# Value-row expansion on GpSimd's queue, a later residual fold, one joined block and edge lists in parts in a fused convolution, attention and graph kernel

## The chip, the cores and the metric

The kernel runs on one core of one Trainium2 chip. The core has five engines with a queue of instructions each: TensorE (PE, matmuls and transposes), VectorE (DVE), ScalarE (ACT), GpSimd (POOL) and SyncE (SP). DMAs are issued from the queues of SP, ACT and POOL. The metric is the device time of one execution in microseconds (us); lower is better.

## The reference, cut to what matters

The input is x, 8 images of 56 x 56 pixels with 64 channels, in float32. Three layers follow one another.

```python
# layer 0: 32 paths, each 1x1 to 4 channels, 3x3, 1x1 back to 64 (batch norm and relu after each)
x = relu(sum_over_paths(path(x)) + x)
t = x.reshape(8, 3136, 64)
# layer 1: attention with 8 heads of 8, each pixel over its 7 x 7 neighbourhood
t = t + attention(layernorm(t))
# layer 2: a graph of 262144 random edges over the first 16384 tokens gives each token
# scores for 4 experts (softmax over incoming edges); the best 2 experts are mixed
t = t + experts(layernorm(t), gates(graph_attention(layernorm(t), edges)))
```

## The kernel before, in words

**Stages.** `build_program` writes the program as a sequence of blocks. At the end of a block all engines meet, and `clear` sets the semaphores of the stage to zero in a block of its own. (1) `conv_part` for images 0 to 5 (EARLY = 6), with the sort of the edge list beside it. (2) `attention_part` for the first 74 strips of four image rows (14 strips an image), with `Index`, which finds the place of every node in the sorted list. (3) `table_part`, 16 steps of 8 x 128 tokens: layer norm, and from it a table with a row per node. (4) One large block: POOL issues 1 + 128 + 2048 indirect DMAs (`Edge.gathers`); beside them run `conv_part` for images 6 and 7, the other 38 strips, the rest of the table, the experts' matmuls, and on VectorE the scans over the 16 chunks of edges. (5) `finish_phase` gathers the sums, computes the gates and mixes the outputs.

**The convolution.** An image has 7 tiles of 8 rows (448 pixels), so stage 1 has 42 tiles g. For a tile, `expand` on TensorE (L541 and on) runs 16 chunks c: a matmul of 448 columns of the stack into psE (L563), two chunks to a pair ("duo"), with two psE buffers. VectorE adds each pair with a relu into acc (L892 for the first pair of a tile, L895 for the other seven). Between the chunks TensorE does the nine taps of the 3x3 convolution of tile g + 3 at chunks 4 to 12 (L541), transposes for the sort (L278), and for earlier tiles the functions in `others`: at FOLD_AT `to_tokens` of tile g - 1 (the fold, L587, which waits for that tile's last addition into acc and writes psF), at TURN_AT the transposes of z of tile g - 2 (L598), at PROJECT_AT the projection to q, k, v (L604, L610). On VectorE `rest` (h2r, L870) stands ahead of pair 0 and `last_part` (L875, which waits for ScalarE's copy L676) ahead of pair 1; `residual` (usum, L834) after pair 1 waits for the fold. SORT_SLOTS lists, for each of eleven steps of the sort in a tile, the chunk at which it stands; on VectorE a step stands ahead of pair chunk // 2, and a transpose of the sort follows chunk - 1 on TensorE. ScalarE's order in a tile: relu, z, the copies of the split, then (`turned`) the z of tile g - 2 out of PSUM, then the nine DMAs that load the stack of tile g + 2.

**SP's queue in the convolution.** In loop g it issues the load of x_ch of tile g + 7 (L415; three buffers, waits for the matmul L531 that read the old one), x_tok of tile g + 2 (L420), the stores of t1 of tile g - 1 and of q, k, v of tile g - 2 (L461, L462, L466). Once an image, at g = 10, 17, and so on, and once at the end, `widen(n)` follows: it waits until the image's value rows have been stored to vpad, and issues ten DMAs DRAM to DRAM (L475), one for each key column kx, each of 62 rows x 14 blocks with a run of 64 float32; they make vwin, in which attention finds the rows of values of a strip in one piece. After the last widening SP stores the sorted edge list (L497) and waits for everything, all widenings among it.

**Attention.** SP loads the sorted keys (`index.load`, L1253), waits for three memsets on VectorE (`zeroed`: wproj, and the two q_exp), loads the constants (L987), then q, keys, values and t1 of strip after strip. TensorE scores (L1053), VectorE takes the minimum (L1163), ScalarE the exponentials, and so on. VectorE first computes the digits of the index (L1262 to L1271). After the third strip `Index` counts, and POOL gathers keys with 128 indirect DMAs (L1305).

**The table and the edge lists.** VectorE writes `out`, 4 MB of edge lists (16 chunks), in steps 0 to 5 of the table's loop. `store_edges` on SP at step 8 stores all of it to `edge_dram` in one DMA (L1320), and `load_edges` at step 11 reads the first four chunks back into `edge`. In stage 4 the list of chunk c + 4 is loaded when chunk c has been scanned (L1684), and POOL waits for it before it gathers for chunk c + 4.

## Time and profile before

| | us |
|---|---|
| median of 3 runs | 5194.17 |
| lowest and highest of them | 5192.73, 5196.02 |
| the profiled execution | 5185.15 |
| its span, first to last instruction | 5183.3 |
| busy: PE, DVE, ACT, POOL | 2531.1, 2425.5, 1507.2, 2512.5 |

All rows below are of the one profiled execution, in its own time; a time "at 1201.5" is microseconds from the start of its span. A queue's row (SPq) gives the time in which the queue was issuing, not that in which the data moved. Engines are in order: an instruction that waits holds all behind it.

### The profile page before, as it was taken

The numbers are of one execution on the slowest core, as the hardware profiler recorded it, in microseconds if no ns is written. First come the engines' busy times: TensorE is split into PE (matmuls) and PEld (weight loads), VectorE is DVE, ScalarE is ACT, GpSimd is POOL, SyncE is SP. The second block draws the span as 40 slices with busy tenths as digits, with TensorE's granted clock in tenths as the row PEclk, the third lists the DMA queues.
The fourth block names the chain that finished last, engine by engine and source line by source line (L and its number), as shares of the span: only waits on it lengthen the run. The fifth ranks groups of instructions, "written<-read, shape, count | busy, mean of one in ns | idle before, by whom it ended". The sixth has DMA issues, their size and how long they took to land. (4 is left out here: it accounts for less than half of the span.)

```text
span 5183.3 us, 45952 instructions
## 1 busy us (share of the span) xinstructions
PE 2531.1 (49%) x13822; PEld 1705.6 (33%) x13822; DVE 2425.5 (47%) x3759; ACT 1507.2 (29%) x5754; POOL 2512.5 (48%) x2477
## 2 busy tenths in 40 slices
PE   5777687771999975783695530122202220122032
PEld 2444344441888863441684310000000000000022
DVE  6887686782799972441598411011101111011187
ACT  1333232321788831231584220011101110011000
POOL 1000000000460024777777777777777777777564
PEclk8787787875899965775797575666556665566566
DMA  4556455442444423663443321111101111111144
GB/s 93 96 111 126 105 101 104 100 78 69 99 114 103 103 74 91 91 100 59 91 111 86 89 61 13 40 45 44 44 8 45 44 44 22 29 42 42 33 165 149
DMA packets 585938, 397.27 MB, mean 77 GB/s; under 512 B 399291, under 2 KB 513003, under 8 KB 582491
## 3 DMA queue, kind: packets, MB, share of 16 engines
q1 hardware_dynamic: 411920, 259.22, 19.3%
q10 hardware_dynamic: 95819, 110.02, 10.8%
q0 software_dynamic: 77952, 25.09, 4.9%
q8 instruction: 112, 1.84, 0.1%
q14 instruction: 135, 1.11, 0.1%
HBM read 251.02 MB, written 160.83 MB: 79 GB/s over the span
## 5 line engine op out<-in xcount | busy, mean ns | idle before, releaser
L1665 POOL DMA_INDIRECT e_row<-scratch_table,k_edge x2048 | 2024.1, 988 | 681.2 <-issue 681.2
L1819 PE MATMUL f_psY<-f_hid,f_w 128*128 128x512 f32 x392 | 207.2, 677 | 1414.7 <-ACT f_hid L1780 1414.7
L1708 DVE TENSOR_TENSOR e_e<-e_row,e_b 128x512 f32<-128x512 f32 x16 | 11.2, 697 | 1709.1 <-DMA e_row<-scratch_table,k_edge 1709.0
L1305 POOL DMA_INDIRECT i_keys<-scratch_ordered,i_group_ix x128 | 148.6, 1161 | 1364.3 <-DVE i_group_ix L1298 1322.5
L1819 PEld LDWEIGHTS f_psY<-f_hid,f_w 128*128 128x128 f32 x392 | 80.5, 216 | 1539.2 <-issue 1530.7
L1125 ACT ACTIVATE prob<-psS,low 128x100 f32<-128x100 f32 x1568 | 512.4, 372 | 60.1 <-DVE low L1163 54.3
L541 PE MATMUL psH<-h,c_w 128*128 128x448 f32 x1008 | 513.2, 601 | 8.3 <-ACT h L664 4.6
L1053 PE MATMUL psS<-keys,q_exp 84*128 84x100 f32 x3136 | 399.2, 279 | 194.0 <-DMA keys<-in_kfeat 189.8
L1734 ACT ACTIVATE e_weight<-e_drop 128x1024 f32<-128x1024 f32 x16 | 16.9, 1056 | 1608.8 <-DVE e_drop L1717 1608.8
L895 DVE SCALAR_TENSOR_TENSOR acc<-psE,acc 128x896 f32<-128x896 f32 x392 | 425.9, 1087 | 71.3 <-PE psE L563 66.6
L563 PE MATMUL psE<-stack,c_w 75*128 75x448 bf16 x896 | 357.1, 443 | 196.9 <-DVE acc L895 171.3
L1053 PEld LDWEIGHTS psS<-keys,q_exp 84*128 84x128 f32 x3136 | 385.1, 200 | 194.7 <-issue 194.7
L1125 ACT ACTIVATION_READ_ACCUMULATOR prob<-psS,low 128x1 f32 x1568 | 369.4, 236 | 0.0
L541 PEld LDWEIGHTS psH<-h,c_w 128*128 128x128 f32 x1008 | 218.4, 218 | 138.7 <-issue 128.5
L1067 PE MATMUL psP<-a_ident,prob 128*100 128x128 f32 x1568 | 227.5, 286 | 48.3 <-ACT prob_t L1136 41.6
L1163 DVE TENSOR_REDUCE low<-psS 128x5 f32<-128x500 f32 x336 | 214.6, 642 | 73.3 <-PE psS L1053 66.3
L1136 ACT ACTIVATE prob_t<-psP 100x512 f32<-100x512 f32 x448 | 227.6, 581 | 53.0 <-PE psP L1067 53.0
L563 PEld LDWEIGHTS psE<-stack,c_w 75*128 75x128 bf16 x896 | 96.4, 118 | 409.6 <-issue 210.7
L1444 POOL TENSOR_TENSOR t_sq<-t_cen 128x512 f32<-128x512 f32 x16 | 17.5, 1095 | 393.5 <-DVE t_cen L1530 393.5
L587 PE MATMUL psFV<-c_fold,acc 128*112 128x64 f32 x896 | 172.8, 383 | 58.8 <-DVE acc L895 48.4
L1079 PE MATMUL psO<-prob_t,val 100*64 100x128 f32 x3136 | 200.4, 280 | 1.9 <-issue 1.9
L1067 PEld LDWEIGHTS psP<-a_ident,prob 128*100 128x100 f32 x1568 | 161.1, 130 | 96.3 <-ACT prob_t L1136 59.1
(287 smaller groups left out, 4619.2 us busy)
## 6 DMA issues: line engine op xcount, KB each, us to landing
stack<-scratch_parts ACTq DMA_DIRECT2D x504, 112.0 KB
val<-scratch_vwin SPq DMA_DIRECT2D x112, 350.0 KB
e_row<-scratch_table,k_edge POOLq DMA_INDIRECT x2048
scratch_y<-f_y ACTq DMA_DIRECT2D x49, 512.0 KB
scratch_state<-e_state SPq DMA_DIRECT2D x16, 1536.0 KB, 6.3
g_y<-scratch_y SPq DMA_DIRECT2D x24, 1024.0 KB
scratch_parts<-h2p ACTq DMA_DIRECT2D x56, 336.0 KB, 5.2
scratch_vwin<-scratch_vpad SPq DMA_DIRECT2D x80, 217.0 KB
```

What stands on the lines that cost most here:

```text
L541: m = pe.matmul(psH2[:, 0:PIX].rearrange("p (y x) -> p y x", x=W), w2[:, tap, :], h1[:, ROWS * t + dy:ROWS * (t + 1) + dy, dx:dx + W], sta ...
L563: m = pe.matmul(psE[duo % 2][:, half, 0:PIX], w3[:, c, :], stack[third(n, t)][:, c, :], start=True, stop=True)
L587: m = pe.matmul(psF[0:TOK, s * C:(s + 1) * C], acc[:, third(n, t), half, s * TOK:(s + 1) * TOK], fold[:], start=(half == 0), stop=(half == 1))
L895: dve.scalar_tensor_tensor(acc[:, third(n, t)], e, 0.0, acc[:, third(n, t)], ALU.max, ALU.add).then_inc(stt_done, 1)
L1053: m = pe.matmul(psS[bank][:, (blk - a) * KEYS:(blk - a + 1) * KEYS], q_exp[st.pair][:, par, blk].rearrange("k h m -> k (h m)"), keys[st.at ...
L1067: m = pe.transpose(psP[k % 2][0:KEYS, (blk - a) * 128:(blk - a + 1) * 128], prob[par][:, blk * KEYS:(blk + 1) * KEYS], ident[:])
L1079: m = pe.matmul(psO[part][half * C:(half + 1) * C, (blk - a) * 128:(blk - a + 1) * 128], val[st.at][:, half * HALF + blk, :], prob_t[:, ha ...
L1125: m = act.activation(prob[par][:, blk * KEYS:(blk + 1) * KEYS], psS[bank][:, (blk - a) * KEYS:(blk - a + 1) * KEYS], ACT.Exp, bias=low[par ...
L1136: act.activation(prob_t[:, a:b, :], psP[k % 2][0:KEYS, 0:(b - a) * 128].rearrange("k (b m) -> k b m", m=128), ACT.Copy).then_inc(pt_done, 1)
L1163: dve.tensor_reduce(low[par][:, a:b], psS[bank][:, 0:(b - a) * KEYS].rearrange("p (b k) -> p b k", k=KEYS), AX.X, ALU.min)\
L1665: pool.indirect_dma_start(out=self.row[s][:, f, :], out_offset=None, in_=table_dram[0:NODES], in_offset=bass.IndirectOffsetOnAxis(ap=keep. ...
L1819: m = pe.matmul(psY[par][:, e // 2, :], w2[:, e, :], hid[e][:], start=e % 2 == 0, stop=e % 2 == 1)
```

## The change

The widening of an image is issued from POOL's queue in stage 1, as a list of 60 DMAs behind POOL's memsets, with a semaphore `widened[n]` for each image. The convolution no longer waits for it; attention's load of values waits for the semaphore of its image. In stage 4 SP keeps the widening, two DMAs in each of five tiles for image 6, and for image 7 one in each of ten strips of attention. The fold goes from chunk 0 to chunk 3, the transposes of z from 3 to 6, and the first slot of the sort from 4 to 5. Stages 1 to 3 become one block: attention's engines wait for a semaphore `conv_over` of SP, and the table's for `attention_over`; one `clear` at the end takes all semaphores. Two of the three memsets ahead of attention go to POOL, behind its wait for `conv_over`. The first four chunks of the edge list are copied from `out` to `edge` by SP directly, and ScalarE stores the whole list in four parts of 1 MB, after its steps 8, 10, 12 and 14.

```diff
-SORT_SLOTS = (4, 5, 6, 7, 8, 9, 10, 11, 12, 13, 14)
+SORT_SLOTS = (5, 5, 6, 7, 8, 9, 10, 11, 12, 13, 14)
-FOLD_AT, TURN_AT, PROJECT_AT = 0, 3, 13
+FOLD_AT, TURN_AT, PROJECT_AT = 3, 6, 13
...
+        def widen(eng, n, kx):
+            last = n * TILES + TILES - 1
+            if kx == 0:
+                for g in range(last - 2, last + 1):
+                    eng.wait_ge(qkv_stored[g % 3], 64 * (g // 3 + 1))
+            rows = vpad_dram[image0 + n]
+            eng.dma_start(vwin_dram[image0 + n, :, kx],
+                          bass.AP(rows.tensor, rows.offset + kx * C, [[PW * C, PH], [QCOLS * C, BLOCKS], [1, C]])).then_inc(widened[image0 + n], 16)
...
-                if g >= TILES + 3 and (g - 3) % TILES == 0:
-                    widen((g - 3) // TILES - 1)
-            widen(N - 1)
+                if not prologue and TILES + 3 <= g < TILES + 8:
+                    for kx in range(2):
+                        widen(sp, 0, 2 * (g - TILES - 3) + kx)
...
-            sp.wait_ge(widened, 16 * WIN * N)
             if over is not None:
                 sp.sem_inc(over, 1)
...
+                for n in range(N):
+                    for kx in range(WIN):
+                        widen(pool, n, kx)
...
             def load_val(st):
                 n, s = of(st)
                 wait(sp, pv_ready, 2 * st.i - 6)
+                if n >= image0:
+                    sp.wait_ge(widened[n], 16 * WIN)
...
+                if late is not None and 2 <= i < 2 + WIN:
+                    late(sp, i - 2)
...
             def _(pool):
+                pool.wait_ge(begin, 1)
+                pool.memset(wproj[:], 0.0).then_inc(zeroed, 1)
+                pool.memset(q_exp[1][:], 0.0).then_inc(zeroed, 1)
                 index.gather_keys(pool)
...
-            dve.memset(wproj[:], 0.0).then_inc(zeroed, 1)
-            for a in q_exp:
-                dve.memset(a[:], 0.0).then_inc(zeroed, 1)
+            if index is None:
+                dve.memset(wproj[:], 0.0).then_inc(zeroed, 1)
+                dve.memset(q_exp[1][:], 0.0).then_inc(zeroed, 1)
+            dve.memset(q_exp[0][:], 0.0).then_inc(zeroed, 1)
...
-        sp.dma_start(self.edge_dram.rearrange("k p d f -> p k d f"), self.out[:]).then_inc(self.edge_stored, 16)
-
-    def load_edges(self, sp, edge, edge_in):
-        sp.wait_ge(self.edge_stored, 16)
         for s in range(AHEAD):
-            sp.dma_start(edge[s][:], self.edge_dram[s]).then_inc(edge_in[s], 16)
+            sp.dma_start(edge[s][:], self.out[:, s]).then_inc(edge_in[s], 16)
+
+    def store_part(self, act, j):
+        if j == 0:
+            act.wait_ge(self.limits, 1)
+        act.dma_start(self.edge_dram[4 * j:4 * j + 4].rearrange("k p d f -> p k d f"), self.out[:, 4 * j:4 * j + 4]).then_inc(self.edge_stored, 16)
...
-                if index is not None and k == 11:
-                    index.load_edges(sp, keep.edge, edge_in)
...
+                sp.wait_ge(index.edge_stored, 16 * NFC // 4)
...
+                if index is not None and i in (8, 10, 12, 14):
+                    index.store_part(act, i // 2 - 4)
...
                 with nc.Block() as block:
-                    conv_part(nc, block, stage, conv_weights, io, 0, EARLY, True, t1, q, kpad, vpad, vwin, ordered, b)
-                clear(nc, stage.all)
...
-                with nc.Block() as block:
-                    attention_part(nc, block, stage, io, 0, EARLY_STRIPS, t1, q, kpad, vwin, t2, index=index)
-                with nc.Block() as block:
+                    conv_part(nc, block, stage, conv_weights, io, 0, EARLY, True, t1, q, kpad, vpad, vwin, ordered, b, widened, over=conv_over)
+                    index = Index(nc, ctx, stage, soft, keep, io, ordered, edge_rows, node, first, ends)
+                    attention_part(nc, block, stage, io, 0, EARLY_STRIPS, t1, q, kpad, vwin, t2, widened, index=index, begin=conv_over, over=attention_over)
+
+                    @block.vector
+                    def _(dve):
+                        dve.wait_ge(attention_over, 1)
...
                     table_part(nc, block, stage, conv_weights, keep, io, 0, NODES // 128, True, t2, z, table, adst, index=index, edge_in=edge_in)
                 clear(nc, stage.all)
```

## Rows read from the trace of the kernel before

**Rows 1.** Busy time by stage: us, each engine's busy us, PEclk, DMA share, GB/s

```profile
core 0: us, PE busy (x) PEld busy (x) DVE busy (x) ACT busy (x) POOL busy (x), PEclk, DMA share, GB/s
78.00:1180.00 1102.00, 807.30 (x2887) 454.39 (x2885) 860.56 (x1016) 340.59 (x1213) 0.00 (x0) 0.76 0.53 101
...
1867.00:2004.00 137.00, 86.61 (x384) 75.41 (x384) 69.67 (x123) 24.95 (x81) 45.41 (x32) 0.50 0.41 113
2004.00:4883.00 2879.00, 988.70 (x4648) 598.07 (x4648) 705.75 (x1268) 622.38 (x2017) 2152.23 (x2177) 0.64 0.26 53
```

**Rows 2.** Waits of POOL: us in total, times, longest us

```profile
POOL e_row L1665 <- issue: 681.2, 2048, 7.9
```

**Rows 3.** Line 1665: duration ns min/median/max, first and last start

```profile
L1665 POOL DMA_INDIRECT e_row<-scratch_table,k_edge x2048: 940/944/3370, 2177.7 to 4881.8; - x187
```

**Rows 4.** Waits of all engines from 0 to 1260

```profile
DVE acc L892 <- PE psE L563: 191.6, 42, 29.5
...
PE psH L531 <- DMA x_ch<-in_x_ch: 75.3, 4, 25.8
...
DVE usum L834 <- DMA x_tok<-in_x: 4.7, 1, 4.7
```

**Rows 5.** SP's queue in order of time: start, us, what

```profile
352.33 79.03 SPq L475 DMA_DIRECT2D scratch_vwin<-scratch_vpad  x10
431.41 6.17 SPq L415 DMA_DIRECT2D x_ch<-in_x_ch  x1
```

**Rows 6.** SP's queue around the convolution's end

```profile
1201.52 55.66 SPq L475 DMA_DIRECT2D scratch_vwin<-scratch_vpad  x10
1257.22 6.03 SPq L497 DMA_DIRECT2D scratch_ordered<-sort_other  x1
1272.67 0.35 SPq L1253 DMA_DIRECT2D i_key<-scratch_ordered  x1
...
1280.44 0.33 SPq L987 DMA_DIRECT2D a_ident<-in_ident  x1
```

**Rows 7.** VectorE at the end of a tile and the start of the next

```profile
224.29 1.08 DVE L895 SCALAR_TENSOR_TENSOR acc<-psE,acc 128x896 f32<-128x896 f32 x1
...
226.43 1.08 DVE L895 SCALAR_TENSOR_TENSOR acc<-psE,acc 128x896 f32<-128x896 f32 x1
...
227.71 0.63 DVE L870 TENSOR_TENSOR h2r<-h,h2p 128x448 f32<-128x448 f32 x1
231.23 1.09 DVE L892 TENSOR_SCALAR acc<-psE 128x896 f32<-128x896 f32 x1 [2.89 <-PE psE L563]
```

**Rows 8.** TensorE at the same place

```profile
227.57 3.25 PE L587 MATMUL psFV<-c_fold,acc 128*112 128x64 f32 x16 [1.51 <-DVE acc L895]
```

**Rows 9.** ScalarE at the same place

```profile
229.17 0.56 ACT L676 ACTIVATE h2p<-h2r 128x448 bf16<-128x448 f32 x1
```

**Rows 10.** VectorE in the first tile

```profile
77.77 1.09 DVE L892 TENSOR_SCALAR acc<-psE 128x896 f32<-128x896 f32 x1 [7.80 <-PE psE L563]
```

**Rows 11.** TensorE at the start of attention

```profile
1294.04 6.27 PE L1053 MATMUL psS<-keys,q_exp 84*128 84x100 f32 x28 [97.27 <-DMA keys<-in_kfeat]
```

**Rows 12.** VectorE at the start of attention

```profile
1300.31 1.73 DVE L1163 TENSOR_REDUCE low<-psS 128x5 f32<-128x500 f32 x3
```

**Rows 13.** DMA issues by line, whole span: KB each, us to landing

```profile
i_key<-scratch_ordered SPq DMA_DIRECT2D x1, 1024.0 KB, 4.7
```

**Rows 14.** POOL at the start of the program

```profile
2.50 2.90 POOL L513 MEMSET h<- 128x3364 f32 x1
```

**Rows 15.** VectorE's waits in the first table

```profile
DVE t_stat L1522 <- DMA t_t<-scratch_t: 19.8, 3, 17.4
```

**Rows 16.** SP's queue in the third stage

```profile
2824.65 0.43 SPq L1684 DMA_DIRECT2D k_edge<-scratch_edge  x1
```

**Rows 17.** Line 1665 alone from 2004 to 2831: POOL busy and count

```profile
2004.00:2831.00 827.00, 493.69 (x476) 0.76 0.47 85
```

**Rows 18.** DMA queues, 1205 to 1256: packets, MB, share of 16 engines

```profile
q1 hardware_dynamic: 7230, 1.85, 15.9%
```

More of the change, by code:

```diff
@@ L467, in store_qkv @@
                                  v[r * W:(r + 1) * W, g % 3]).then_inc(qkv_stored[g % 3], 16)
-            def widen(n):
-                last = n * TILES + TILES - 1
-                for g in range(last - 2, last + 1):
-                    sp.wait_ge(qkv_stored[g % 3], 64 * (g // 3 + 1))
-                rows = vpad_dram[image0 + n]
-                for kx in range(WIN):
-                    sp.dma_start(vwin_dram[image0 + n, :, kx],
-                                 bass.AP(rows.tensor, rows.offset + kx * C, [[PW * C, PH], [QCOLS * C, BLOCKS], [1, C]])).then_inc(widened, 16)
             if prologue:
@@ L911, in _, with attention_part @@
                 sort_at[at]()
-def attention_part(nc, block, lasting, io, lo, hi, t1_dram, q_dram, kpad_dram, vwin_dram, t2_dram, index=None, begin=None, over=None):
+def attention_part(nc, block, lasting, io, lo, hi, t1_dram, q_dram, kpad_dram, vwin_dram, t2_dram, widened, index=None, begin=None, over=None, late=None):
     with ExitStack() as ctx:
-        tag = f"_{lo}"
+        tag = f"_a{lo}"
         sb = lambda name, shape, dt=F32: ctx.enter_context(nc.sbuf_tensor(name + tag, shape, dt))
@@ L922, in attention_part @@
         COUNT = hi - lo
+        image0 = EARLY if late is not None else 0
         HALF = BLOCKS // 2
@@ L2217, in build_program @@
             conv_weights, keep = ConvWeights(nc, whole), Keep(nc, whole)
+            widened = [soft(f"v_widened{n}") for n in range(EARLY)]
             edge_in = [soft(f"e_edge_in{i}") for i in range(AHEAD)]
@@ L2221, in build_program, with _ @@
                 stage = Semaphores(nc, ctx)
+                conv_over, attention_over = stage("conv_over"), stage("attention_over")
                 with nc.Block() as block:
-                    conv_part(nc, block, stage, conv_weights, io, 0, EARLY, True, t1, q, kpad, vpad, vwin, ordered, b)
-                clear(nc, stage.all)
-            with ExitStack() as ctx:
-                stage = Semaphores(nc, ctx)
-                index = Index(nc, ctx, stage, soft, keep, io, ordered, edge_rows, node, first, ends)
-                with nc.Block() as block:
-                    attention_part(nc, block, stage, io, 0, EARLY_STRIPS, t1, q, kpad, vwin, t2, index=index)
-                with nc.Block() as block:
+                    conv_part(nc, block, stage, conv_weights, io, 0, EARLY, True, t1, q, kpad, vpad, vwin, ordered, b, widened, over=conv_over)
[4 more added lines that the diff above has]
+                        dve.wait_ge(attention_over, 1)
+                    @block.scalar
+                    def _(act):
+                        act.wait_ge(attention_over, 1)
+                    @block.tensor
+                    def _(pe):
+                        pe.wait_ge(attention_over, 1)
+                    @block.gpsimd
+                    def _(pool):
+                        pool.wait_ge(attention_over, 1)
                     table_part(nc, block, stage, conv_weights, keep, io, 0, NODES // 128, True, t2, z, table, adst, index=index, edge_in=edge_in)
@@ L2239, in build_program @@
                 conv_over, attention_over, table_over = stage("conv_over"), stage("attention_over"), stage("table_over")
+                widened_late = [None] * EARLY + [stage(f"v_widened{n}") for n in range(EARLY, IMAGES)]
                 with nc.Block() as block:
@@ L2243, in _, with late @@
                         edge.gathers(pool, table, adst, b)
-                    conv_part(nc, block, stage, conv_weights, io, EARLY, IMAGES - EARLY, False, t1, q, kpad, vpad, vwin, ordered, b, over=conv_over)
-                    attention_part(nc, block, stage, io, EARLY_STRIPS, IMAGES * STRIPS, t1, q, kpad, vwin, t2, begin=conv_over, over=attention_over)
+                    conv_part(nc, block, stage, conv_weights, io, EARLY, IMAGES - EARLY, False, t1, q, kpad, vpad, vwin, ordered, b, widened_late, over=conv_over)
+                    def late(sp, kx):
+                        rows = vpad[IMAGES - 1]
+                        sp.dma_start(vwin[IMAGES - 1, :, kx],
+                                     bass.AP(rows.tensor, rows.offset + kx * C, [[PW * C, PH], [QCOLS * C, BLOCKS], [1, C]])).then_inc(widened_late[IMAGES - 1], 16)
+                    attention_part(nc, block, stage, io, EARLY_STRIPS, IMAGES * STRIPS, t1, q, kpad, vwin, t2, widened_late, begin=conv_over, over=attention_over, late=late)
                     edge.tiles(nc, ctx)
```

10 lines of the change are left out of this document (5 added, 5 removed).

## The prediction

> **What bounds the kernel now.** I read the span cut into its stages first [rows 1]: the first convolution (six images, 78 to 1180), its tail and the first attention (to 1867, not shown as a row), the first table (to 2004), the third stage (to 4883); the finish fills the rest. In the third stage GpSimd (POOL) issues 2177 indirect DMAs. The waits of POOL [rows 2] show that its 681.2 us of idle time before the 2048 edge gathers wait for nothing but their own issue (0.33 us each, 7.9 us at most), and one gather takes 944 ns as a rule [rows 3]. So POOL's list sets the length of that stage: whatever the change saves on the second convolution and attention is hidden there, and whatever it saves before 2004 comes off the end one for one. The whole question is what happens before the first gather.
>
> The waits of that part [rows 4] name two losses. VectorE (DVE), busy 78% of the first convolution [rows 1], waits 191.6 us in 42 tiles for the first pair of expansions of a tile (L892), and TensorE (PE) waits 75.3 us, four times, for x_ch. The SyncE (SP) queue shows why x_ch is late: the ten DMAs of one image's widening hold the queue for 79.0 us, and the next x_ch load leaves only behind them [rows 5]. The last image's ten stand alone at the end: they hold SP from 1201.5 for 55.7 us, and attention's first load goes out at 1272.7 [rows 6].
>
> **The change part by part.** All terms are differences to the profiled execution.
>
> *Widening moved to POOL, inside the convolution.* SP loses 60 issues; its loads and stores behind them are no longer held. The reader of x_ch runs about three tiles of some 25 us behind the load, so a hold of 80 us is just too long and none at all is ample: the 75.3 us go [rows 4]. Some of those waits could have been covered anyway by DVE, whose own loss is what counts: 65 as the lower end, 75 the value, as DVE waits along. The x_tok wait at the end (4.7 us, [rows 4]) goes as well, but the fold before it, which PE can't start earlier, ends 3 us into it: 2 us.
> By a rule of the Trainium skill ("DMA: Bandwidth & Descriptors", section Issuing engines are not separate DMA queues) all issued DMAs run on the same 16 engines, and another issuing engine saves only the issue time, usually small. Here the issue time is not small; what the rule would give is rival one.
>
> *The fold three chunks later.* Take an ordinary tile [rows 7]: DVE ends the last addition at 227.5 and the remainder (h2r) at 228.3, then waits 2.89 us until 231.2, because PE had to wait for that last addition, then fold (from 227.57, [rows 8]), then expand. After the change chunks 0 and 1 precede the fold and need only the addition before, which ended at 225.4; DVE goes on at 228.3. What is late next: the last part of the split needs ScalarE's copy, which ends at 229.7 [rows 9], 0.3 us after DVE would want it (228.34 + 1.09); and the residual wants the fold. Chunks 2 and 3 start at 227.5 and take some 0.8 us (one chunk now reaches DVE 0.41 us after the fold's end at 230.82), the fold 3.25, so it is there at 231.6 to 231.8; DVE, after 0.6 for the last part and 1.09 for the pair, comes to it at 231.4: 0.2 to 0.4 us. Left per tile 0.7, or 0.3 where the fold is quicker. Now the sum: of the 191.6 us the first tile's 7.8 [rows 10] stay and the 75.3 are counted above, so 108.5 us belong to 41 folds, 2.65 each; less 41 x 0.7 = 29 leaves 80. Upper end 41 x 0.3 left: 96. Lower end: in tiles with transposes of the sort PE has little to spare and the wait moves to the second pair; half of 2.65 lost on average leaves about 50. The later transposes of z (chunk 6) delay ScalarE's stack loads by about 3 us; these are wanted over a tile later, and PE waits elsewhere for DVE. The slot of the sort moved from 4 to 5 stays in the same pair of chunks on DVE; on PE it stays behind the fold. Both cost nothing.
>
> *The tail and the joined block.* Before: loads of attention's constants wait for three memsets on DVE and leave at 1280.4 [rows 6]; 13.6 us later PE scores [rows 11]; the first minimum comes at 1300.3, when DVE has done its 20 us of digits [rows 12]. After, on the same clock: the last value rows have landed by 1201.5 (SP's widening waited for exactly that). The sorted list goes out at once instead of at 1257; 1 MB takes about 4.7 us [rows 13], so conv_over comes at about 1204. DVE clears one q_exp, loads of the key land by 1209, and digits end near 1229. But two memsets are now POOL's, queued behind the ten widening DMAs of the last image: if one issue costs w, they end at 1201.5 + 10w + 3.4 (a POOL memset of like size took 2.90, [rows 14]), and the first minimum comes 13.6 + 2.2 later, at 1220.7 + 10w, or at 1229 if that is later. The trace shows no direct DMA on POOL, so w has bounds from the gathers [rows 3]: 0.94 + 0.30 of issue for 128 rows, so 1.24 if rows cost nothing; a widening DMA has 868 runs of 256 B (62 rows x 14 blocks), so 6.7 if rows cost everything. SP's own 5.57 per DMA lies between. No row is nearer to one end, so I take the middle, w = 4: first minimum at 1261, a gain of 39. Ends: 67 and 12. POOL's other fifty issues (at 6.7 us, 67 us of the 158 of an image: 1102 less 155, over six) hide beside the convolution, where POOL is idle [rows 1].
>
> *Edge lists in parts.* Before, one 4 MB store makes the table's loads late: DVE waits 17.4 us once [rows 15]. After, 1 MB goes SBUF to SBUF at step 8 and four stores of 1 MB are spread over steps 8 to 14, issued by ScalarE (four issues, some 2 us, in a stage where it is busy 25 of 137 us [rows 1]). The first two megabytes still meet: I take 10 back; ends 3 and 17. The readback of four chunks, about 2 us of issues on SP, falls away too; the store must land before the stage ends, and has 20 us to.
>
> *Blocks.* The block end with its clear took 4.7 us after the convolution (from 1263.3, when the sorted list was issued, less 4.7 for its landing, to 1272.7, [rows 6, 13]). The clearing moves to the end of the table: it costs 0 to 4.7 there. A block end after attention goes: 0 to 2 back. Together -1.5, ends -4 and +2.
>
> *Third stage.* Its widening is spread over SP, two per tile and one per strip. POOL would notice only if the reload for chunk 4 came late: it leaves SP at 2824.7 [rows 16] and lands by 2831, when POOL has issued 476 of the 512 gathers before it [rows 17]; 36 x 1.25 = 45 us of cover, and the 57 us hold of the last widening before that goes, so the cover grows. Nothing.
>
> Sum: 75 + 2 + 80 + 39 + 10 - 1.5 = 204.5. The profiled execution took 5185.15 us (span 5183.3), the median of the runs is 9 us above it (5194.17): 5185.15 - 204.5 + 9 = 4990. All best ends: 75 + 4 + 96 + 67 + 17 + 2 = 261, 4933; all worst: 65 + 0 + 50 + 12 + 3 - 4 = 126, 5068.
>
> **The rivals.**
> *One: the transfers, not the queue, make x_ch late.* The widening still runs beside the loads on the same DMA engines. For it: its DMAs move only 36 GB/s alone. Against it: alone they fill 15.9% of the engines [rows 18], and x_ch left SP 79 us late. The 75 stay: 5065. Chance 0.07.
> *Two: the fold's wait only changes place* (to the residual or the second pair of expansions). For it: PE is busy 73% of the stage. Against: in the tile shown PE itself waits 1.51 us just ahead of the fold [rows 8], and it waits for DVE again wherever the sort runs. The 80 stay: 5070. Chance 0.08.
> *Three, on the other side: generation on POOL is slow,* and the memsets at the end of its list hold attention. Sixty issues start near 280 us and run to 280 + 60w; the memsets were done at 1280 before, and the rest saves about 10, so from w = 17 us the kernel is no faster, and at 20 us it is 180 us slower: about 5375. For it: beside busy engines single gathers took up to 3.37 us [rows 3], which times 868/128 would be 23 us. Against: their median stays at 0.944. Chance 0.04.
> The Trainium skill speaks for this one ("SBUF — State Buffer", section SBUF: two separate sides): while VectorE runs an operation in a two-port mode, GpSimd can't write its descriptors, and it advises SP or ACT for such DMAs. No row here shows a direct DMA on POOL beside the sort.
> *Four: the third stage takes it back,* POOL waiting for chunk 4 because attention ends over 45 us later after the first gather than now; every us beyond costs one, and all is lost at 250. The second convolution has less on its queue, so I give 0.02.
>
> **How the numbers follow.** My forecast has 0.79: 4990, with 4933 to 5068 as its own range. Rivals one and two end at its upper edge. The unknown w alone moves the time by 27 to either side, the fold by 15 to 30, the edge store by 7. All ends of one kind together are unlikely, so 8 in 10 lies within 4940 to 5070. Within 0.2% (10 us) counts as no change, about what a measurement of this kernel can tell. Faster: the forecast, rivals one and two, and part of four: 0.95; same 0.01; slower 0.04.
>
> **What would show it.** Right: no wait of PE for x_ch; DVE's wait at L892 near 0.7 us a tile, and tiles without transposes some 2.3 us shorter; the first gather of the third stage near 1800 and the gathers still without another wait; POOL's widening issues between 1.2 and 6.7 us, and the first minimum as far behind the last value store as 10w + 19 us says. Wrong: long waits at L834 for the fold or at the second pair (L895); POOL issues of over 10 us; a POOL wait for k_edge in the third stage; x_ch or stack loads landing late while POOL's queue is full.

## The result, and the profile after

The changed kernel takes 5118.23 us (median of 4 runs, 5112.96 to 5121.66) where the kernel before takes 5195.10 on the same chip: ratio 0.9851, 95% interval 0.9834 to 0.9868. That is 77 us faster; 205 were forecast, and 5118 lies above the range. The profiled execution took 5115.46 us, its span 5113.6, so 69.7 us of span are to be accounted for.

Some fixed points cut both spans into stretches: VectorE's first pair of a tile (L892 before, L894 after), TensorE's first score, GpSimd's first square and last z of the table, and its first gather. All but the medians is read from one profiled execution of each kernel.

| stretch | before | after | gain | forecast |
|---|---|---|---|---|
| to the first pair of the first tile | 77.8 | 79.2 | -1.4 | 0 |
| 41 tiles, first pair to first pair | 1086.7 | 1009.0 | 77.6 | 157 |
| to the first score | 129.6 | 134.5 | -4.9 | 39 |
| attention, to the table's first square | 579.9 | 584.7 | -4.8 | 0 |
| to the table's last z | 107.5 | 100.5 | 7.0 | 10 |
| to the first gather | 22.9 | 27.0 | -4.1 | -1.5 |
| to the end of the span | 3179.0 | 3178.7 | 0.2 | 0 |

Two rows carry the miss: 79 us in the convolution, 44 behind it. First the waits of all engines from 0 to 1260 (us in total, times, longest), beside [rows 4]:

```profile
POOL scratch_vwin L405 <- issue: 432.6, 24, 29.3
ACT sq_c L704 <- issue: 260.5, 37, 21.1
...
DVE stat_c L845 <- ACT sq_c L704: 74.5, 18, 11.3
...
DVE h2p_c L877 <- ACT h2p_c L678: 24.4, 41, 3.4
...
DVE acc_c L894 <- PE psE_c L565: 14.1, 6, 10.5
...
DVE usum_c L836 <- PE psFV_c L589: 8.6, 11, 3.1
```

The squares' row of the kernel before:

```profile
DVE stat L843 <- ACT sq L702: 7.7, 6, 2.7
```

What the change was to remove is gone: no engine waits for x_ch or x_tok, and VectorE's wait for the first pair fell from 191.6 to 14.1 us. New is the third line: the variance (of the layer norm behind the convolution) waits 74.5 us for ScalarE's squares; before, that was 7.7. The 67 us between are most of the 79 missing in the convolution. The second line says what the squares wait for: nothing but the issuing in front of them. The longest tile, 37.9 us, shows it. These are its rows from 396 to 423 us (start, us, what; queues, ScalarE, VectorE and TensorE one after the other):

```profile
399.26 5.59 POOL L405 DMA_DIRECT2D scratch_vwin<-scratch_vpad  x2 [17.30 <-issue]
```
```profile
396.16 4.70 SPq L454 DMA_DIRECT2D scratch_vpad<-c_zero_c  x2
400.90 2.61 SPq L458 DMA_DIRECT2D scratch_b<-c_zero_c  x1
403.55 3.79 SPq L424 DMA_DIRECT2D x_ch_c<-in_x_ch  x1
```
```profile
399.04 18.44 ACTq L689 DMA_DIRECT2D stack_c<-scratch_parts_c  x9
417.59 0.35 ACT L704 ACTIVATE sq_c<-t_c,stat_c 112x64 f32<-112x64 f32 x1 [21.07 <-issue]
```
```profile
419.05 0.17 DVE L845 TENSOR_SCALAR stat_c<-stat_c 112x4 f32<-112x4 f32 x1 [11.35 <-ACT sq_c L704]
```
```profile
422.76 0.91 PE L565 MATMUL psE_c<-stack_c,c_w 75*128 75x448 bf16 x2 [13.50 <-DVE acc_c L897]
```

ScalarE issues the nine stack loads of a tile in about 3.3 us where GpSimd is quiet; here it is held for 18.4. The squares stand behind them, the variance behind the squares, the tile's last two additions behind the variance, TensorE behind those. SyncE's single issues also take 3.8 us instead of 0.5. The short issues, from the same run before the first widening:

```profile
207.00 3.32 ACTq L689 DMA_DIRECT2D stack_c<-scratch_parts_c  x9
```
```profile
195.25 0.49 SPq L424 DMA_DIRECT2D x_ch_c<-in_x_ch  x1
```

This longest tile is not the widening's alone. From 399 to 417.5 us the 16 DMA engines are 90% busy, mostly with SyncE's transfers, the zero fills among them. Below, q1 is SyncE's queue, q0 GpSimd's with the widening, q10 ScalarE's with the stack loads (packets, MB, share of 16 engines):

```profile
q1 hardware_dynamic: 678, 2.20, 61.5%
q0 software_dynamic: 640, 0.31, 17.9%
q10 hardware_dynamic: 606, 0.52, 10.6%
```

So tiles away from the widening take 22.9 us (25.3 before, as forecast), those beside it up to 38.

Then the tail. GpSimd after the convolution (first block), SyncE and TensorE:

```profile
1126.48 5.59 POOL L405 DMA_DIRECT2D scratch_vwin<-scratch_vpad  x2 [21.35 <-DMA scratch_vpad<-v_c]
1145.16 5.58 POOL L405 DMA_DIRECT2D scratch_vwin<-scratch_vpad  x2 [13.09 <-issue]
...
1196.14 5.59 POOL L405 DMA_DIRECT2D scratch_vwin<-scratch_vpad  x2 [11.36 <-issue]
1201.77 0.21 POOL L1119 MEMSET a_wproj_a<- 128x128 f32 x1
1201.91 3.10 POOL L1120 MEMSET q_exp_a<- 84x3584 f32 x1
```
```profile
1123.38 0.42 SPq L497 DMA_DIRECT2D scratch_ordered<-sort_other_c  x1
...
1205.03 0.33 SPq L990 DMA_DIRECT2D a_ident_a<-in_ident  x1
```
```profile
1222.68 6.27 PE L1060 MATMUL psS_a<-keys_a,q_exp_a 84*128 84x100 f32 x28 [101.60 <-DMA keys_a<-in_kfeat]
```

The last image's list begins at 1126.5 and ends at 1201.7: w, the price of a DMA on GpSimd's queue, is 7.5 us here. An issue itself takes 2.8; after every pair GpSimd sits some 11 to 13 us before it issues again. The trace shows what it waits for: in each of the 24 places where one pair follows another within an image, the next issue starts 0.34 us after the second DMA of the pair has landed. From 1126 to 1205 us the ten take, from issue to landing:

```profile
DMA to landing us min/median/max: 10.7/13.3/15.6
```

So w is set by the time in which a pair lands, not by the time in which GpSimd issues it. The memsets follow, and the constants leave SyncE 82 us after the sorted list.

### The profile page after: what moved, and what is told of

Read it like the earlier page. It is cut to its first block and busy times, and to the rows that moved or that the text cites. A ratio compares the mean times of both kernels' runs of the same rounds, so it can differ in the third digit from the quotient of the medians.

```text
span 5113.6 us, 46024 instructions
## 1 busy us (share of the span) xinstructions
PE 2557.7 (50%) x13822; PEld 1737.0 (34%) x13822; DVE 2428.5 (47%) x3757; ACT 1511.7 (30%) x5754; POOL 2685.4 (53%) x2539
## 5 line engine op out<-in xcount | busy, mean ns | idle before, releaser
L1721 DVE TENSOR_TENSOR e_e<-e_row,e_b 128x512 f32<-128x512 f32 x16 | 11.2, 701 | 1748.5 <-DMA e_row<-scratch_table,k_edge 1748.4
L1135 ACT ACTIVATE prob_a<-psS_a,low_a 128x100 f32<-128x100 f32 x1568 | 512.5, 371 | 62.2 <-DVE low_a L1174 58.1
L543 PE MATMUL psH_c<-h_c,c_w 128*128 128x448 f32 x1008 | 524.6, 613 | 8.6 <-ACT h_c L666 4.9
L1060 PE MATMUL psS_a<-keys_a,q_exp_a 84*128 84x100 f32 x3136 | 417.2, 287 | 173.9 <-DMA keys_a<-in_kfeat 162.2
L565 PE MATMUL psE_c<-stack_c,c_w 75*128 75x448 bf16 x896 | 356.5, 444 | 237.5 <-DVE acc_c L897 211.0
L897 DVE SCALAR_TENSOR_TENSOR acc_c<-psE_c,acc_c 128x896 f32<-128x896 f32 x392 | 426.2, 1087 | 81.2 <-PE psE_c L565 77.6
L1060 PEld LDWEIGHTS psS_a<-keys_a,q_exp_a 84*128 84x128 f32 x3136 | 402.8, 207 | 175.8 <-issue 175.7
L1135 ACT ACTIVATION_READ_ACCUMULATOR prob_a<-psS_a,low_a 128x1 f32 x1568 | 367.6, 234 | 0.0
L543 PEld LDWEIGHTS psH_c<-h_c,c_w 128*128 128x128 f32 x1008 | 223.3, 222 | 136.5 <-issue 126.0
L1074 PE MATMUL psP_a<-a_ident_a,prob_a 128*100 128x128 f32 x1568 | 234.1, 291 | 47.2 <-ACT prob_t_a L1146 39.7
L1146 ACT ACTIVATE prob_t_a<-psP_a 100x512 f32<-100x512 f32 x448 | 227.4, 578 | 92.0 <-PE psP_a L1074 91.7
```

Of the source, the lines that this page charges most:

```text
L543: m = pe.matmul(psH2[:, 0:PIX].rearrange("p (y x) -> p y x", x=W), w2[:, tap, :], h1[:, ROWS * t + dy:ROWS * (t + 1) + dy, dx:dx + W], sta ...
L565: m = pe.matmul(psE[duo % 2][:, half, 0:PIX], w3[:, c, :], stack[third(n, t)][:, c, :], start=True, stop=True)
L897: dve.scalar_tensor_tensor(acc[:, third(n, t)], e, 0.0, acc[:, third(n, t)], ALU.max, ALU.add).then_inc(stt_done, 1)
L1060: m = pe.matmul(psS[bank][:, (blk - a) * KEYS:(blk - a + 1) * KEYS], q_exp[st.pair][:, par, blk].rearrange("k h m -> k (h m)"), keys[st.at ...
L1074: m = pe.transpose(psP[k % 2][0:KEYS, (blk - a) * 128:(blk - a + 1) * 128], prob[par][:, blk * KEYS:(blk + 1) * KEYS], ident[:])
L1135: m = act.activation(prob[par][:, blk * KEYS:(blk + 1) * KEYS], psS[bank][:, (blk - a) * KEYS:(blk - a + 1) * KEYS], ACT.Exp, bias=low[par ...
```

## Experiments

Medians in us; before is the kernel before, run on the same chip. "Tiles" is the 41 tiles' stretch, "squares" VectorE's wait for them (0 to 1260), both from the one profiled execution of each run.

| run | median | before | ratio (95%) | tiles | squares |
|---|---|---|---|---|---|
| changed kernel | 5118.2 | 5195.1 | 0.9851 (0.9834 to 0.9868) | 1009.0 | 74.5 |
| e1 fold alone | 5174.2 | 5199.5 | 0.9952 (0.9936 to 0.9969) | 1051.8 | 13.9 |
| e2 without the fold | 5189.3 | 5199.5 | 0.9979 (0.9969 to 0.9988) | 1079.5 | 55.4 |
| e3 SyncE, in parts | 5017.4 | 5199.5 | 0.9656 (0.9639 to 0.9672) | 939.4 | 13.6 |
| e4 stack loads on SyncE | 5047.8 | 5199.5 | 0.9710 (0.9693 to 0.9726) | 937.5 | 1.5 |
| e5 memsets on VectorE | 5068.4 | 5193.5 | 0.9750 (0.9726 to 0.9775) | 1026.6 | 85.1 |
| e6 fills early | 5107.9 | 5193.5 | 0.9843 (0.9811 to 0.9876) | 998.8 | 39.2 |
| e7 before, block by block | 5058.8 | 5193.5 | 0.9741 (0.9725 to 0.9758) | 1013.9 | 1.5 |
| e8 e3, block by block | 4954.2 | 5193.5 | 0.9550 (0.9529 to 0.9571) | 925.9 | 5.8 |
| e9 changed, block by block | 4982.5 | 5196.0 | 0.9600 (0.9584 to 0.9616) | 945.0 | 18.6 |
| e10 e4 and e5 | 4988.1 | 5196.0 | 0.9603 (0.9587 to 0.9620) | 943.6 | 1.5 |
| e11 e7 and e1 | 4983.5 | 5195.1 | 0.9590 (0.9563 to 0.9617) | 931.7 | 6.7 |
| e12 edges in one store | 5121.3, one run | 5195.1 | | 1009.6 | 68.0 |

**The fold with and without GpSimd's widening.** e1 is the kernel before with these lines, e2 the changed kernel without them:

```diff
-SORT_SLOTS = (4, 5, 6, 7, 8, 9, 10, 11, 12, 13, 14)
+SORT_SLOTS = (5, 5, 6, 7, 8, 9, 10, 11, 12, 13, 14)
-FOLD_AT, TURN_AT, PROJECT_AT = 0, 3, 13
+FOLD_AT, TURN_AT, PROJECT_AT = 3, 6, 13
```

> The kernel before with the later fold, the later transposes and the sort slot alone; widening, blocks and edge store as before. Tiles away from the widening of the changed kernel take 22.9 us where they took 25.3, so the fold is worth 2.4 x 41 = 98 us. Theory (ScalarE's queue held by the stack loads while GpSimd's widening runs costs the 75 us that are missing): no widening on GpSimd here, so the 98 come, less some 29 because SyncE's 79 us hold now covers three tiles that are each 2.4 us shorter, four times: 5195 - 70 = 5125, and VectorE's waits of its variance for the squares under 20 us. Rival (the transposes of z at chunk 6 make ScalarE's stack loads and squares late whatever widens): the 75 us of waits for the squares show up here too: about 5200.

> The changed kernel with the fold at chunk 0, the transposes at 3 and the sort slot at 4 again; widening stays on GpSimd. Theory (stack loads held on ScalarE's queue beside GpSimd's widening): the waits for the squares stay near 75 us and the 2.65 us idle of each tile comes back, 98 to 108 in all where they do not overlap: 5118 + 98 = 5216, at least 5170. Rival (the later transposes are the cause): the fold's 98 are lost, but the 75 of the squares come back: about 5141, and the variance waits under 20 us.

In e1 the tiles gained only 34.9 us, because waits grew behind SyncE's hold of the shorter tiles:

```profile
PE psH L531 <- DMA x_ch<-in_x_ch: 110.9, 4, 33.5
...
DVE stat L843 <- ACT sq L702: 13.9, 6, 4.3
...
DVE usum L834 <- DMA x_tok<-in_x: 13.4, 1, 13.4
```

110.9 less 75.3 and 13.4 less 4.7 are 44.3; with 34.9 the fold is worth 79, not the 98 expected. From the last tile's first pair to the first score e1 lost another 10 us (139.7 for 129.6). So 25 us were gained where 70 were expected. But the waits for the squares are small here and stay at 55.4 us in e2: the later transposes are not the cause, GpSimd's widening is. In e2 it leaves 7 us in the tiles: it removes 75 us of waits for x_ch and brings most of them back as waits for the squares.

**The queue.** e3 puts the first stage's widening back on SyncE, two DMAs per tile, the last image's in the strips of attention:

```diff
-                if not prologue and TILES + 3 <= g < TILES + 8:
+                m, k = divmod(g - TILES - 3, TILES)
+                if 0 <= m < N - 1 and k < 5:
                     for kx in range(2):
-                        widen(sp, 0, 2 * (g - TILES - 3) + kx)
+                        widen(sp, m, 2 * k + kx)
...
-                for n in range(N):
-                    for kx in range(WIN):
-                        widen(pool, n, kx)
...
```

> The changed kernel with the widening of the first stage on SyncE again, two DMAs per tile in five tiles (the last image one DMA per strip of the first attention), GpSimd issues none. The bytes are the same and GpSimd's pace was two DMAs per 20 to 28 us too, so only the queue differs. Theory (GpSimd's route is what holds ScalarE's stack loads): all tiles near 22.9 us, -75; the tail gains too, since conv_over no longer finds memsets behind ten DMAs, first score about 25 us behind the last value store where it was 96: -70; together 5118 - 145 = 4973. Rival (any widening beside the convolution costs its transfers): the tiles beside it stay near 27 us and only the tail gains: 5048. Second rival (two DMAs of 5.6 to 8 us on SyncE's queue per tile make x_ch late again): waits of TensorE for x_ch over 30 us.

The tiles came down to 939.4 us, as the theory says, with squares at 13.6 and no wait for x_ch; the transfers alone do not cost 75 us. The total missed by 44: the tail gained 63, attention's strips, held by the last image's DMAs, took 602.7 us where 584.7 was the comparison, the stretch from the first gather on took 6 more, and the median stands 10 us above the profiled execution.

**The order on ScalarE's queue.** e4 issues the stack loads from SyncE:

```diff
-                    if not (last and t + 2 >= TILES):
+                    if not prologue and not (last and t + 2 >= TILES):
                         stack_parts(*ahead(n, t, 2))
...
                 if 1 <= g <= ALL:
                     store_t1(g - 1)
+                if prologue and g < ALL - 2:
+                    r = (g + 2) % 3
+                    sp.wait_ge(parts_out[r], 16 * ((g + 2) // 3 + 1))
+                    for j in range(3):
+                        for i in range(3):
+                            at = (3 * j + i) * HC
+                            sp.dma_start(stack[r][at:at + HC], by_chunk(parts_dram[r, :, i])).then_inc(stacked[r], 16)
```

> The changed kernel with the nine stack loads of a tile issued by SyncE, ahead of its stores of q, k and v, where ScalarE issued them ahead of the squares; widening stays on GpSimd. Theory (in-order hold: the squares are late because they stand behind the held issues, and the stack itself is in time): VectorE's wait for the squares falls from 74.5 us to under 15, tiles beside the widening go from 27 to 23 to 24 us: 5118 - 70 = 5048. Rival (the stack's data come late with the slow transfers): the wait moves to TensorE for the stack loads, 60 us or more, and the time stays within 20 us of 5118.

5047.8 for 5048 expected, and 1.5 us of waits for the squares are left. The loads are still slow beside the widening (nine took 10.3 us on SyncE's queue at 412.7, and TensorE waits 25.0 us in all for a stack, 10.6 in the changed kernel), but little stands behind them. So the waits for the squares come from held issues in front of them, not from late data; without them the tiles are 71.5 us shorter.

**The tail.** e5 leaves all three memsets to VectorE:

```diff
                 pool.wait_ge(begin, 1)
-                pool.memset(wproj[:], 0.0).then_inc(zeroed, 1)
-                pool.memset(q_exp[1][:], 0.0).then_inc(zeroed, 1)
...
-            if index is None:
-                dve.memset(wproj[:], 0.0).then_inc(zeroed, 1)
-                dve.memset(q_exp[1][:], 0.0).then_inc(zeroed, 1)
+            dve.memset(wproj[:], 0.0).then_inc(zeroed, 1)
+            dve.memset(q_exp[1][:], 0.0).then_inc(zeroed, 1)
```

> The changed kernel with all three memsets ahead of attention on VectorE, as in the kernel before; widening stays on GpSimd, five pairs of it alone after the convolution. Theory (the memsets queued behind the last image's ten DMAs hold attention): the constants leave SyncE at once, the first score comes some 25 us behind the last value store (now 96), the widening of the last image runs beside the first strips: 5118 - 65 = 5053. Rival (its transfers now hold the loads of the first strips, as they hold the stack loads in the convolution): half of it is given back in the first six strips, 5085. Second rival (digits and constants set the start, not the memsets): over 5110.

From the last tile's first pair to the first score: 75.3 us instead of 134.5, and attention took 576.3, so the strips paid nothing. The median still missed by 15: the convolution, in which nothing was changed, took 1026.6 in this profile for 1009.0, and the runs spread from 5052 to 5078. The waits for the squares, 85.1 us here and 74.5 there, suggest that the hold varies from one execution to the next.

**Do the zero fills bring it about?**

```diff
             if prologue:
-                clear_pads(0)
+                for n in range(IMAGES):
+                    clear_pads(n)
...
-                if prologue and g >= 2 and (g - 2) % 5 == 0 and (g - 2) // 5 + 1 < IMAGES:
-                    clear_pads((g - 2) // 5 + 1)
-                if prologue and g >= 8 and g - 8 < EDGES * GHEADS // (C * ZEROS):
-                    clear_b(g - 8)
+                if prologue and g < EDGES * GHEADS // (C * ZEROS):
+                    clear_b(g)
```

> The changed kernel with the zero fills moved: the pads of all eight images are cleared before the first tile and the edge list's b in tiles 0 to 7, where they stood at every fifth tile and in tiles 8 to 15; same bytes, widening on GpSimd as it is. In the changed kernel the five longest tiles (37.9, 34.7, 29.6, 28.5, 34.3 us) stand at the pads' fills at 393, 514, 641 and 892 us, which meet a widening; the fill at 772 meets none and its tiles take 21.6 and 24.7. Theory (it needs both: the fills' long transfers beside the widening hold ScalarE's stack loads): tiles beside the widening fall to 23 to 25 us, waits for the squares from 74.5 to under 25, 5118 - 55 = 5063. Rival (the widening through GpSimd's queue is enough by itself): the waits stay over 55 us and the time within 20 us of 5118. A price at the start, where 15 MB are written beside the first tiles, is possible: up to 15 us.

Neither. The tile of 37.9 us became 25.7, the waits for the squares halved to 39.2, the tiles from the second on gained 28 us; the start lost 31 (first pair at 92.3, then a first tile of 42.2 us; TensorE waits 23.9 for a stack). Two places show each cause by itself: the nine stack loads beside the fills, before any widening, and beside the widening, with no fill in flight; below the second, the DMA queues from 327 to 338 us:

```profile
63.77 19.88 ACTq L688 DMA_DIRECT2D stack_c<-scratch_parts_c  x9
```
```profile
326.93 11.24 ACTq L688 DMA_DIRECT2D stack_c<-scratch_parts_c  x9
```
```profile
q0 software_dynamic: 737, 0.36, 41.8%
q10 hardware_dynamic: 400, 0.34, 27.1%
```

So the widening holds ScalarE's issues by itself, and dense fills do too; in the changed kernel's longest tiles both met.

**The order of the runs.** Each widening DMA has 868 runs of 256 B. e7 is the kernel before with their order turned, e9 the changed kernel, e8 is e3:

```diff
-                    sp.dma_start(vwin_dram[image0 + n, :, kx],
-                                 bass.AP(rows.tensor, rows.offset + kx * C, [[PW * C, PH], [QCOLS * C, BLOCKS], [1, C]])).then_inc(widened, 16)
+                    sp.dma_start(vwin_dram[image0 + n, :, kx].rearrange("y b c -> b y c"),
+                                 bass.AP(rows.tensor, rows.offset + kx * C, [[QCOLS * C, BLOCKS], [PW * C, PH], [1, C]])).then_inc(widened, 16)
```

> The kernel before with one change: each widening DMA from SyncE goes through its 868 runs of 256 B block by block (14 blocks of 62 rows) where it went row by row (62 rows of 14 blocks); same bytes, same runs. Before, one issue takes 5.6 us and alone moves 36 GB/s with 15.9% of the engines, about 2.5 of 16. Theory (the outer dimension decides over how many engines a DMA spreads, and SyncE's issue takes as long as those few engines need): with 14 it spreads over 14 engines, ten issues take under 20 us, the four waits for x_ch (75.3 us) fall under 10 and the hold at the end from 55.7 to about 12: 5195 - 70 - 42 = 5083. Rival (the issue time goes by the number of runs): no change, 5195.

> The widening on SyncE in parts (as in e3) and block by block (as in e7). e3 gave 5017: its convolution is at 22.9 us per tile, but its two DMAs per tile hold SyncE 8 to 13 us, its tail is 14 us longer for them, its first attention takes 602.7 us where the changed kernel takes 584.7, and its third stage 6 us more. Theory (these are SyncE's holds): they go, 5017 - 14 - 18 - 6 = 4979. Rival (spread over all engines the widening holds ScalarE's stack loads as GpSimd's does): VectorE's waits for the squares over 40 us, 5030 or more.

> The changed kernel with GpSimd's widening DMAs (and SyncE's in the third stage) going through their runs block by block, as e7 did on SyncE's queue, where this took an issue of ten from 79 to 13 us. Theory (it is the queue: what GpSimd issues slows the stack loads whatever the order of its runs): VectorE's waits for the squares over 55 us, the pairs after the convolution at 15 us or more each, time within 25 us of 5118. Rival (it is the order of the runs, on either queue): the waits under 25 us and the ten DMAs after the convolution done in 30 us where they took 75: 5118 - 50 - 45 = 5023.

One statement of the kernel before, turned, gives more than the whole change. The queue of e7, and its DMA queue from 1129 to 1138 us, when the last image's ten run alone, beside [rows 5, 18]:

```profile
353.55 13.18 SPq L475 DMA_DIRECT2D scratch_vwin<-scratch_vpad  x10
366.77 4.06 SPq L415 DMA_DIRECT2D x_ch<-in_x_ch  x1
```
```profile
DMA packets 6500, 1.64 MB, mean 182 GB/s; under 512 B 6500, under 2 KB 6500, under 8 KB 6500
...
q1 hardware_dynamic: 6500, 1.64, 80.4%
```

The kernel before, from 1205 to 1256 us:

```profile
DMA packets 7230, 1.85 MB, mean 36 GB/s; under 512 B 7230, under 2 KB 7230, under 8 KB 7230
```

80.4% of 16 engines are 12.9, where 15.9% were 2.5; 182 GB/s against 36. Ten issues fall from 79 to 13 us and no wait for x_ch is left. e8, with the turned order wherever rows are widened, is the fastest of all, 4954.2. Both came out faster than expected, e7 by 24 us (its end gained 52 for 42), e8 by 25 (its tiles are 13.5 us shorter than e3's, which was not forecast); the rest of both differences I have not settled.

On GpSimd's queue I expected no effect, and was wrong. e9: GpSimd's queue at the first image, the durations of all its issues (ns, min/median/max), and the wait for the squares; below them the changed kernel's durations:

```profile
298.68 8.20 POOL L405 DMA_DIRECT2D scratch_vwin<-scratch_vpad  x10 [274.92 <-DMA scratch_vpad<-v_c]
```
```profile
L405 POOL DMA_DIRECT2D scratch_vwin<-scratch_vpad x60: 798/803/1431, 298.7 to 1068.7; - x60
```
```profile
DVE stat_c L845 <- ACT sq_c L704: 18.6, 6, 4.5
```
```profile
L405 POOL DMA_DIRECT2D scratch_vwin<-scratch_vpad x60: 2795/2797/3032, 299.7 to 1198.9; - x60
```

0.80 us an issue instead of 2.80, ten in a row without a pause, tiles of 945.0 us, and the last image's ten issued in 8 us where they took 75. The kernel takes 4982.5, less than the 5023 of the rival that was right. So what holds ScalarE is not GpSimd's queue as such; it is this order of runs on that queue. GpSimd's DMA queue for the last image, in the changed kernel from 1126 to 1214 us and in e9 from 1061 to 1085 us (packets, MB, share of 16 engines):

```profile
q0 software_dynamic: 4640, 2.47, 38.0%
```
```profile
q0 software_dynamic: 800, 2.23, 29.9%
```

The same image is 4640 packets and 535 us of engine time (0.380 x 16 x 88) the one way, 800 packets and 115 us (0.299 x 16 x 24) the other. By the sizes in the trace, 540 packets of 4 KB and 20 of 512 B make up the whole 2.22 MB of the ten DMAs in the changed kernel. The other packets therefore carry none of the rows, and nearly all of them, 3780, are of 64 B and take 421 of the 535 us. In e9 60 are of 64 B.

**The two holds repaired, and the fold alone again.** e10 joins the edits of e4 and e5, e11 those of e7 and e1.

> The changed kernel with the two repairs that worked alone: the stack loads on SyncE's queue (e4, -70) and the three memsets on VectorE (e5, -50). Theory (these two holds are all that parts the forecast of 4990 from the 5118 measured, and they stand in different places): they add up, 5118 - 70 - 50 = 4998, the convolution's 41 tiles in 937 to 945 us. Rival (they share a cause, or the last image's widening beside attention's first loads takes back what the convolution gains): 5030 or more.

> The kernel before with the widening block by block on SyncE (e7) and the later fold, transposes and sort slot (e1); blocks, memsets and edge store as before. With the fold alone (e1) the 41 tiles gained 35 us, since the waits for x_ch rose by 36 and that for x_tok by 9; in e7 the waits for x_ch are gone. Theory (the fold is worth some 75 to 80 us where nothing else holds the tiles): e7's 41 tiles of 1013.9 us go to about 938, 5059 - 76 = 4983, the same as e9, in which the widening is on GpSimd. Rival (the fold's wait only changes place): tiles over 975 us, 5020 or more.

Both as the theories say. e10, with widening on GpSimd in its slow order, lands at 4988.1, 2 us from the forecast of 4990. That this is so close is luck in part: its tiles take 943.6 us where the forecast implies 929.7 (1086.7 less 157), and its stretch to the first score 75.3 where it implies 90.6 (129.6 less 39). e11 gives the fold its price: 1013.9 less 931.7 is 82 us. And at 4983.5 it equals e9 (4982.5): with the runs in the better order, GpSimd's queue, the joined block and the edge parts together bring nothing over the fold on the kernel before. They do gain, 16 us to the first score and 6 in the table, but the tiles are 13 us longer, and attention, the wait for the first gather and the stretch behind it 4 each.

**The edge store.** e12 is the changed kernel with one store and a read-back:

```diff
-        for s in range(AHEAD):
-            sp.dma_start(edge[s][:], self.out[:, s]).then_inc(edge_in[s], 16)
+        sp.dma_start(self.edge_dram.rearrange("k p d f -> p k d f"), self.out[:]).then_inc(self.edge_stored, 16)
...
+                if index is not None and k == 11:
+                    index.load_edges(sp, keep.edge, edge_in)
...
-                if index is not None and i in (8, 10, 12, 14):
-                    index.store_part(act, i // 2 - 4)
```

> The changed kernel with the edge lists in one store of 4 MB and the read-back, as before. From the table's first square on GpSimd to its last z the kernel before took 107.5 us, the changed one 100.5. Theory (the parts are worth the 7 us that this stretch became shorter): 107 again, with a wait of VectorE for its tile of t of 17 us. Rival (the joined block or the loads' order gave them): 101, and the wait stays near 10.

107.3 us and a longest wait of 17.1: the 7 us are the parts'. It is one run, but the others agree: this stretch took 107.4 to 107.8 us in e1, e7 and e11, which store the list in one piece, and 100.5 to 101.8 in all with parts. VectorE in the table of the changed kernel, then of e12:

```profile
DVE t_stat_t L1533 <- DMA t_t_t<-scratch_t: 14.1, 4, 10.4
```
```profile
DVE t_stat_t L1533 <- DMA t_t_t<-scratch_t: 19.4, 3, 17.1
```

## Why the prediction was wrong, step by step

**The step that failed** is the half sentence that GpSimd's other fifty issues "hide beside the convolution, where POOL is idle". It asked only whether the issuing engine has time. Its DMAs lengthened the issues of ScalarE and SyncE, ScalarE's nine stack loads above all, and squares, variance and expansion queue in order behind these. The tiles miss 79 of the 123 us that are missing in the two rows of the table; taking the stack loads off ScalarE's queue gives 71.5 of them back (e4), the widening on SyncE in parts 69.6 (e3), the turned order on GpSimd 64 (e9). What the last 8 to 15 are is not shown. I had cost the stack loads only for the later transposes. My signs of being wrong name "stack loads landing late while POOL's queue is full", but no price stands against them, and e4 shows that it was the issuing, not the landing, that cost the time.

**The second failure has the same root: w.** The formula for the tail held: 10 x 7.5 + 19 = 94 us from the last value rows to the first minimum, 98.7 measured (1126.5 to 1225.2). But w was bounded by 1.24 and 6.7 from what an issue costs GpSimd, and the issue itself, 2.8, is inside. The pause after each pair, until it has landed, is not in it; the gathers, from which the bounds came, wait 0.33 us for one another on average (681.2 over 2048, [rows 2]). At w = 7.5 instead of 4 the list is 35 us longer. The tail lost 4.9 where 39 were forecast (1.1 if it is counted to the first minimum, for which the 39 were worked out); e5 gives 59 back by taking the memsets out from behind the list.

**Right:** the waits for x_ch: 72.8 us by e7's tiles, with the waits gone, for 65 to 75. The fold: 82 us (e11) for 80, with (24.4 + 8.6) / 41 = 0.8 us left per tile for 0.7, the 24.4 at ScalarE's copy and the 8.6 at the residual. Edge parts 7 for 10, ends 3 and 17. **Blocks:** 25.9 us of wait before the first gather where 21.8 stood, so -4.1, a little beyond the lower end given. **Third stage:** 0.2 for nothing; no wait for k_edge. Attention's 4.8 us were not forecast; the first attention takes 576 to 585 us in e1, e4, e5, e9 and e10 too, and I have not settled what moves it.

**The rivals.** One (transfers make x_ch late) fell: no wait for x_ch anywhere in the change. Its counter-argument, that the DMAs "alone fill 15.9% of the engines", was taken from SyncE's queue; on GpSimd's the same transfers filled 38.0%. Rival one was too narrow: transfers did bring a loss, but through ScalarE's queue. Two fell with e11. Three was right that the memsets at the end of GpSimd's list hold attention, at w = 7.5 instead of 17; but generation was not what was slow (2.8 us), the landing was. The Trainium skill's rule that I cited for it ("SBUF — State Buffer", section SBUF: two separate sides) would make issues slower beside those operations of VectorE that run in a two-port mode. Which of them do, no row shows. The issues took 2.80 us in the median beside VectorE's work in the convolution and after it, 3.03 at most, so no run here shows the rule. Four fell.

**What stays open.** Why a DMA from GpSimd's queue with its rows outermost brings 3780 packets of 64 B an image, nearly six times the packets and over four times the engine time in all, why only two such DMAs are in flight at once where ten went out in a row with the blocks outermost, and whether the held issues of the other queues wait for engines or for room in a queue: no run here separates these. That all 16 engines were busy all the time can't be the whole of it: the 11.2 us of issuing in e6 fell in a stretch with a mean share of 69%.

## What to carry to other kernels

A DMA moved to an idle engine is hidden only if the other queues' issues stay short beside it. Look at what stands in order behind those issues, and price the move by them, not by the idle engine. Before moving a transfer that holds a queue, ask why it holds it: 36 GB/s from 2.5 engines was in the profile of before, and the order of the runs was worth 135 us in one statement. Shortening tiles lengthens the stalls of a hold of fixed length (e1: 75.3 to 110.9 us), so two savings on one stretch are measured together and apart.

## What the runs showed of the hardware

- The same 868 runs of 256 B, ten DMAs from SyncE, take the time of 2.5 engines and 55.7 us with 62 rows outermost, of 12.9 engines and 9.3 us with 14 blocks outermost. The Trainium skill has a rule for it ("DMA: Bandwidth & Descriptors", section Why a DMA increments its semaphore by 16 and not by 1): a DMA is split over the largest number of engines, 16 at most, that divides the outermost sizes, which gives 2 and 14 here. The two rows bear it out in size, not exactly: 12.9 is a little under 14, but 2.5 is more than 2 (the share adds up the times of packets, and two to four are under way at once in the first row).
- From GpSimd the order changes the issue (2.80 or 0.80 us), the packets (4640 or 800 for an image), the landing (13.3 or 6.3 us in the median, behind the convolution) and how the queue goes on: with the rows outermost the third DMA left only when the two before it had landed, 0.34 us later.
- Beside such a transfer and the zero fills one issue of SyncE took 3.8 us instead of 0.5 and nine of ScalarE 18.4 instead of 3.3; beside the transfer alone the nine took up to 11.2, beside the fills alone up to 20.2 (e6). In these runs issuing had no fixed price of the issuing engine.
